# Subtracting the maxima in attention on TensorE, with sums on VectorE and norm offsets on GpSimd, in a two-layer transformer block

## The reference, cut to what matters

```
x = x + xattn0(layernorm(x), ctx)     # 16 heads of 16, 77 keys, softmax
x = x + ffn0(layernorm(x))            # layernorm(t + relu(t @ w1 + b1) @ w2 + b2) * gamma + beta
x = x + xattn1(layernorm(x), ctx)     # norms both inputs, one head of 256, softmax
x = x + ffn1(x_norm)                  # one of 8 matrices per position, chosen by a router
# xattn0, per head:
scores  = q @ k.T * 0.25
weights = softmax(scores)             # exp(scores - max) / sum
out     = weights @ v
# ffn1: idx = argmax_t(pe @ sign(tile_sigs).T); out = x_norm @ W[idx].T + b[idx]
```

## Time and profile before

| | us |
|---|---|
| median of 3 executions | 313.17 |
| lowest, highest | 312.77, 313.40 |
| span of the profiled execution | 314.0 |
| busy in it: TensorE | 267.9 |
| VectorE | 254.8 |
| ScalarE | 181.7 |
| GpSimd | 157.3 |

### The profile page before, as it was taken

How to read it: one execution, slowest core, us unless ns; L and a number is a source line. 1 busy time by engine, 2 the same in 40 slices (tenths; PEclk the granted TensorE clock), 3 DMA queues, 4 the chain that set the end, 5 groups by cost and what they waited for, 6 DMA issues and landing times.

```text
span 314.0 us, 6283 instructions
## 1 busy us (share of the span) xinstructions
PE 267.9 (85%) x2080; PEld 232.0 (74%) x2080; DVE 254.8 (81%) x664; ACT 181.7 (58%) x606; POOL 157.3 (50%) x157
## 2 busy tenths in 40 slices
PE   2954958977999998999999989999989999878960
PEld 2743937763999698689789959988878988666850
DVE  2998998972889999998997789899899986875640
ACT  2468628526368857478695857775754471454510
POOL 2253640275225878821652263268766653164854
PEclk9995596995999999999999999999999999997995
DMA  6922010240000372100001000011110000000222
GB/s 177 336 72 77 8 42 25 67 142 27 3 0 3 115 222 51 29 24 2 2 0 35 2 0 2 33 52 51 37 36 0 2 0 1 3 0 34 87 78 73
DMA packets 8797, 15.32 MB, mean 49 GB/s; under 512 B 1270, under 2 KB 6813, under 8 KB 8509
## 3 DMA queue, kind: packets, MB, share of 16 engines
q1 hardware_dynamic: 6845, 9.68, 9.2%
q0 software_dynamic: 1920, 5.25, 5.9%
HBM read 11.77 MB, written 3.15 MB: 48 GB/s over the span
## 4 chain that ended last, share of the span: by engine, by line
PE 37%; DVE 29%; issue 15%; POOL 12%; ACT 3%; DVEq 1%; DMA 1%; POOLq 0%; SPq 0%; ACTq 0%
PE PB L256 16%; PE PB L249 7%; PE PB L460 5%; DVE SM L598 3%; POOL SM L1220 3%; DVE SX L649 3%; DVE SM L609 3%; PE S L365 3%; PE S L377 2%; POOL out_x L1282 2%; DVE WD L837 2%; PE PB L327 2%; POOL RAW L1275 2%; DVE XN L701 2%; POOL HL L1254 2%
## 5 line engine op out<-in xcount | busy, mean ns | idle before, releaser
L1220 POOL TENSOR_TENSOR SM<-SM,nhalf 128x2 f32<-128x2 f32 x40 | 29.4, 737 | 98.4 <-DVE SM L604 97.9
L1060 ACT ACTIVATE E<-S,SX 128x77 f32<-128x77 f32 x128 | 39.5, 340 | 16.8 <-DVE SX L652 16.6
L256 PE MATMUL PB<-XTH,W1H 128*128 128x256 f32 x128 | 38.3, 299 | 3.9 <-issue 2.2
L1254 POOL TENSOR_TENSOR HL<-HF,HH 128x512 fp32r<-128x512 f32 x26 | 34.5, 1335 | 13.6 <-DVE HH L682 12.0
L1094 ACT ACTIVATE HF<-PB,cols 128x256 f32<-128x256 f32 x64 | 26.8, 473 | 20.9 <-PE PB L256 20.6
L256 PE MATMUL PB<-W2H,HH 128*128 128x256 f32 x128 | 37.9, 296 | 1.1 <-DVE HL L688 1.1
L256 PE MATMUL PB<-XTH,W1L 128*128 128x256 f32 x128 | 36.4, 284 | 0.0
L256 PE MATMUL PB<-XTL,W1H 128*128 128x256 f32 x128 | 36.4, 284 | 0.0
L256 PE MATMUL PB<-W2H,HL 128*128 128x256 f32 x128 | 35.8, 280 | 0.0
L256 PE MATMUL PB<-W2L,HH 128*128 128x256 f32 x128 | 35.8, 279 | 0.0
L460 PE MATMUL PB<-WD,XP 128*128 x120 | 29.9, 402 | 0.8 <-issue 0.8
(11 more groups left out here) (188 smaller groups left out, 778.3 us busy)
## 6 DMA issues: line engine op xcount, KB each, us to landing
RAW<-in_w SPq DMA_DIRECT2D x4, 512.0 KB, 5.0
WD<-in_WD SPq DMA_DIRECT2D x2, 1024.0 KB
X<-in_x SPq DMA_DIRECT2D x4, 256.0 KB, 7.1
x<-X SPq DMA_DIRECT2D x4, 256.0 KB, 2.2
bc<-in_rows SPq DMA_DIRECT2D x1, 768.0 KB, 7.3
RAW<-in_w_q SPq DMA_DIRECT2D x1, 256.0 KB, 4.2
Wo<-in_w_o SPq DMA_DIRECT2D x1, 256.0 KB, 7.8
RAW<-in_WqT SPq DMA_DIRECT2D x1, 256.0 KB
```

The source lines that it names most:

```text
L256: t = e.matmul(dst, a, b, start=first and j == 0, stop=last and j == n - 1)
L1060: t = e.activation(Ei[:, h * NK:(h + 1) * NK], P[:, at:at + NK], ACT.Exp, bias=SX[:, i, 2, k:k + 1], accum_out=SX[:, i, 1, k:k + 1])
L1220: e.tensor_tensor(sm(K, g, 9), sm(K, g, 8), nhalf[:, :], ALU.pow).then_inc(s["rs" + K], 1)
L1254: e.tensor_tensor(HL[:, hs, :], HF[:, (4 * g + j) % 3, :, :], f(HH[:, hs, :]), ALU.subtract).then_inc(s["hlP"], 1)
```

## The change

The negated maxima now go through TensorE. `smax` writes them straight from the reduction (`negate=True`) into NM, in columns 0 to 3 and 32 to 35 of a strip of 36. `tM` on TensorE transposes the strip into a bank of PB, `mt` on ScalarE copies it to SBUF as MT, and `sm` on TensorE adds MT times SEL (rows of ones for each head's 77 columns) onto the scores that are still in PSUM. Then one exponential over the whole piece reads PSUM and writes E, for every piece, and VectorE sums E for every piece. The offset of the norms A, B, C and D is made on GpSimd in two products (with -1, then with rs). The 15 offsets of the router FFN are loaded into registers at once (`starts`) on each of three engines, in the middle of the program. RR, NM and mask8 move into a part of XP. All five lists of calls are new, except that of SyncE.

```diff
-def by_head(i, a):
-    return a == 0
...
-        RR = sb("RR", [128, 2, 128])
+        MT = sb("MT", [36, 2, 128], F32R)
+        SEL = sb("SEL", [36, 4 * NK], F32R)
...
+        RR, NM, mask8 = two(XP[:, 1, 0, :]), XP[:, 1, 1, 0:172], XP[:, 1, 1, 176:184]
...
+        def load_starts(e, row, most, at):
+
+            values = nc.values_load_multi_w_load_instructions(EV[0:1, row, 0:NP], engines=[e.engine],
+                                                              min_val=0, max_val=most)[1]
+            for n in range(NP):
+                at[n] = values[n]
...
-                P = hold(("sc", g, i, a), ("S", k), ("ex", n + 1) if by_head(i, a) else ("sub", n // 2 + 1))
+                P = hold(("sc", g, i, a), ("S", k), ("ex", n + 1))
...
+            def tM(g, i, a, p):
+                n = 4 * g + 2 * i + a
+                w.wait_ge(s["m_id"], 1)
+                w.wait_ge(s["mx"], n + 1)
+                P = hold(("tM", g, i, a), ("B", p), ("mt", n + 1))
+                e.transpose(P[0:36, 0:128], NM[:, n % 4 * 36:n % 4 * 36 + 36], ident[:, :]).then_inc(s["tM"], 1)
+
+            def sm(g, i, a):
+
+                n = 4 * g + 2 * i + a
+                w.wait_ge(s["mt"], n + 1)
+                w.wait_ge(s["sel"], 2)
+                P = S4[:, place["sc", g, i, a][1], :]
+                for u in range(2):
+                    own = slice(32 * u, 32 * u + 4)
+                    t = e.matmul(P[:, u * 512:u * 512 + 4 * NK], MT[own, n % 2, :], SEL[own, :],
+                                 start=False, stop=True, skip_group_check=True)
+                t.then_inc(s["sm"], 1)
...
+            def starts():
+                w.wait_ge(s["route2"], 1)
+                load_starts(e, 0, 7 * 256, start)
...
-                    if n not in start:
-                        start[n] = e.value_load(EV[0:1, 0, n:n + 1], min_val=0, max_val=7 * 256)
...
-            keys(0); tA(0, 1); vmat(2); q(0, 3); vrep(0, 0); vrep(1, 1); sc(0, 0, 0, 0); sc(0, 0, 1, 1); r_scores(2)
...
+            keys(0); vmat(1); tA(0, 0); q(0, 2); vrep(0, 0); r_scores(1); sc(0, 0, 0, 0); sc(0, 0, 1, 1); tA(1, 2)
+            vrep(1, 3); tM(0, 0, 0, 0); sm(0, 0, 0); tM(0, 0, 1, 0); q(1, 2); sm(0, 0, 1); sc(0, 1, 0, 0)
...
-                e.scalar_tensor_tensor(out=sm(K, g, 10), in0=sm(K, g, 6), scalar=-1.0, in1=sm(K, g, 9),
-                                       op0=ALU.mult, op1=ALU.mult).then_inc(s["mr" + K], 1)
...
-            def scores(g, i, a):
+            def smax(g, i, a):
                 n = 4 * g + 2 * i + a
                 sv = two(bank("sc", g, i, a))[:, :, 0:4 * NK].rearrange("p u (h k) -> p u h k", k=NK)
-                hs = slice(8 * a, 8 * a + 8)
-                return n, sv, SX[:, i, 0, hs].rearrange("p (u h) -> p u h", u=2), hs
-
-            def smax(g, i, a):
-                n, sv, mx_, hs = scores(g, i, a)
                 w.wait_ge(s["sc"], n + 1)
+                w.wait_ge(s["d"], 6)
                 if g:
-                    w.wait_ge(s["rr"], n - 3)
+                    w.wait_ge(s["tM"], n - 3)
+                e.tensor_reduce(two(NM[:, n % 4 * 36:n % 4 * 36 + 64])[:, :, 0:4], sv, AX, ALU.max,
+                                negate=True).then_inc(s["mx"], 1)
+
+            def ssum(g, i, a):
+                n, hs = 4 * g + 2 * i + a, slice(8 * a, 8 * a + 8)
+                w.wait_ge(s["ex"], n + 1)
+                if g:
                     w.wait_ge(s["tE"], n - 3)
-                step(e.tensor_reduce(mx_, sv, AX, ALU.max))
-                settle()
-                if by_head(i, a):
-                    e.tensor_scalar(SX[:, i, 2, hs], SX[:, i, 0, hs], -1.0, None, ALU.mult).then_inc(s["neg"], 1)
-                else:
-                    e.tensor_tensor(E[:, i, a, 0:8 * NK].rearrange("p (u h k) -> p u h k", u=2, h=4), sv,
-                                    mx_.unsqueeze(3).to_broadcast([128, 2, 4, NK]),
-                                    ALU.subtract).then_inc(s["sub"], 1)
-
-            def ssum(g, i, a):
-                n, sv, mx_, hs = scores(g, i, a)
-                w.wait_ge(s["ex"], n + 1)
-                if not by_head(i, a):
-                    step(e.tensor_reduce(SX[:, i, 1, hs], E[:, i, a, 0:8 * NK].rearrange("p (h k) -> p h k", h=8),
-                                         AX, ALU.add))
-                    settle()
-                e.reciprocal(SX[:, i, 2, hs], SX[:, i, 1, hs]).then_inc(s["rc"], 1)
+                step(e.tensor_reduce(SX[:, i, 0, hs], E[:, i, a, 0:8 * NK].rearrange("p (h k) -> p h k", h=8),
+                                     AX, ALU.add))
+                settle()
+                e.reciprocal(SX[:, i, 1, hs], SX[:, i, 0, hs]).then_inc(s["rc"], 1)
...
+            def mt(g, i, a):
+                n = 4 * g + 2 * i + a
+                w.wait_ge(s["tM"], n + 1)
+                if n > 1:
+                    w.wait_ge(s["sm"], n - 1)
+                e.activation(MT[:, n % 2, :], bank("tM", g, i, a)[0:36, 0:128], ACT.Copy).then_inc(s["mt"], 1)
+
             def ex(g, i, a):
                 n = 4 * g + 2 * i + a
-                Ei = E[:, i, a, 0:8 * NK]
-                if by_head(i, a):
-                    P = bank("sc", g, i, a)
-                    w.wait_ge(s["neg"], n // 2 + 1)
-                    if g:
-                        w.wait_ge(s["tE"], n - 3)
-                    for h in range(8):
-                        at = h // 4 * 512 + h % 4 * NK
-                        k = 8 * a + h
-                        t = e.activation(Ei[:, h * NK:(h + 1) * NK], P[:, at:at + NK], ACT.Exp,
-                                         bias=SX[:, i, 2, k:k + 1], accum_out=SX[:, i, 1, k:k + 1])
-                else:
-                    w.wait_ge(s["sub"], n // 2 + 1)
-                    t = e.activation(Ei, Ei, ACT.Exp)
-                t.then_inc(s["ex"], 1)
+                w.wait_ge(s["sm"], n + 1)
+                if g:
+                    w.wait_ge(s["tE"], n - 3)
+                e.activation(two(E[:, i, a, 0:8 * NK]), two(bank("sc", g, i, a))[:, :, 0:4 * NK],
+                             ACT.Exp).then_inc(s["ex"], 1)
...
             def pc(b, r):
                 w.wait_ge(s["xtd"], 4 * b + min(r, 3) + 1)
-                w.wait_ge(s["route2"], 1)
                 if 8 * b + r > 1:
                     w.wait_ge(s["pr"], 8 * b + r - 1)
+                else:
+                    w.wait_ge(s["tE"], 32)
                 for v in range(1 if r == 7 else 2):
                     n = 2 * r + v
-                    if n not in start:
-                        start[n] = e.value_load(EV[0:1, 2, n:n + 1], min_val=0, max_val=7 * 128)
...
+                if K != "Y":
+                    e.tensor_tensor(sm(K, g, 11), sm(K, g, 6), minus[:, :], ALU.mult).then_inc(s["nm"], 1)
+                    minus_made[0] += 1
+                    w.wait_ge(s["rs" + K], g + 1)
+                    w.wait_ge(s["nm"], minus_made[0])
+                    e.tensor_tensor(sm(K, g, 10), sm(K, g, 11), sm(K, g, 9), ALU.mult).then_inc(s["mr" + K], 1)
```

270 lines of the change are left out of this document (146 added, 124 removed), and 2 rows, old and new, of the table SIGNALS.

## The result

| | before | changed |
|---|---|---|
| median of the runs, us | 313.28 (312.77 to 314.03, 4 runs) | 325.75 (322.65 to 327.83, 4 runs) |
| ratio, 95% interval | | 1.035, 1.029 to 1.040 |
| profiled span, us | 314.0 | 324.8 |

The change makes the kernel slower, by 12.5 us between the medians and by 10.9 us (3.5%) by the ratio. Forecast were 306.5, with 298 to 316 as the range; the time lies outside it. Ratios leave out slow executions (here that of 327.83 us), and the profiled executions of e3, e9, e16 and e18 further down were slow ones, 2 to 4 us above the median of their kernel. Measured again beside later runs the changed kernel took 326.09 us, ratio 1.040 (1.028 to 1.053).

What follows compares the result with a forecast made beforehand. TensorE was taken to bound the kernel from 80 us on, with waits before that and near the end. +7.7 - 13.5 + 3 - 4 = -6.8, from the profiled 314.0 to 307.2, given as 306.5 us; range 298 to 316.

Steps and rivals of the forecast that it cites:

- first 80 us: Early stretch where TensorE waits: three causes of waits relieved, less 2 us of new waits, -13.5 us (-7.5 to -20.3).
- new TensorE work, 22 pieces: Full stretch after the first second-FFN product: transposition and product pair cost 0.35 us a piece, +7.7 us (5.5 to 9.9).
- middle, chain and block of loads: Middle: waits at the second product in eight of 22 pieces, plus the one load of 15 offsets, +3 us (1 to 14).
- end: Last stage: offset waits before six passes go, -2; last group's attention waits go, -2; together -4 us (-1 to -5.5).
- (a): At 48.3 us TensorE idles 4.53 us, VectorE's router product stalling beside GpSimd's low part of the weights; removal -5.5 us.
- (b): At 69.3 and 73.6 us TensorE waits, GpSimd's gathers delaying low parts of the hidden layer; moving them gives -4 us.
- (c): At 24.4 and 30.6 us TensorE waits, with half clock after the first; half of 12 us taken back, -6 us.
- costed at nothing: VectorE's relief beyond 80 us and ScalarE's 47 us lie on engines that do not bound, so are worth nothing.
- Rival 2: Slower: TensorE waits at the second product for ScalarE, deciding from 0.45 us a piece; 323 to 324 us, chance 0.16.
- Rival 1: The port: offset waits pass on to normalizations as GpSimd holds VectorE, early gains shrink; 311 us, chance 0.14.
- signs named ahead: Right if: no long router product, low parts before gathers, first product at 66 to 70 us, short copy waits, last group unheld.
- signs of "wrong": Half clock over 10 us before 60 us; TensorE under 18 of 20 us between 100 and 240; normalizations with waits inside.

Runs made afterwards that it cites:

- e3: Kernel before with only GpSimd's first two low parts of the hidden layer moved ahead of the eight gathers; 317.2 us, ratio 1.002.
- e9: Changed kernel with VectorE and ScalarE loading offsets one at a time through the middle, TensorE in front of its passes; 317.5 us, ratio 1.017.
- e16: e9 with the router's two large VectorE steps and TensorE's rank product back where they stood before the change; 325.0 us, ratio 1.022.
- e18: e9 without the 64 products that add the maxima, transpositions and ScalarE's copies kept; 307.9 us, ratio 0.980.
- e12: Changed kernel, unedited, measured again as reference on the chip of later runs; 326.1 us, ratio 1.040.
- e19: e9 unedited, measured again as reference on the chip of later runs; 317.4 us, ratio 1.024.
- e11: e9 without the transpositions of the maxima, their copies and the added products, maxima computed but unused; 305.2 us, ratio 0.979.
- e2: Kernel before with the block of 15 offset loads on TensorE, VectorE and ScalarE in place of single loads; 320.4 us, ratio 1.012.
- e14: Kernel before with VectorE and ScalarE loading offsets one at a time in the middle, not ahead of the passes; 316.7 us, ratio 1.001.
- e1: Changed kernel with the block of loads undone on all three engines, each offset loaded in front of its pass; 327.4 us, ratio 1.035.
- e17: e9 with no maxima at all: no reductions, transpositions, copies or added products; 305.9 us, ratio 0.982.
- e13: e9 with the softmax of the kernel before, new order and spread loads kept; 324.0 us, ratio 1.023.
- e5: New softmax put into the order of the kernel before, offsets loaded one by one; 346.2 us, ratio 1.087.

## Why the prediction was wrong, step by step

| step | forecast | measured |
|---|---|---|
| first 80 us | -13.5 (-7.5 to -20.3) | -12.4 (82.6 to 70.2 in e12; -10.4 in the first profile) |
| new TensorE work, 22 pieces | +7.7 (5.5 to 9.9) | +9.0 (e19 against e11) |
| middle, chain and block of loads | +3 (1 to 14) | +11.7: the block 10.9 to 11.0 (e12 against e9, e19), 0.7 for the rest |
| end | -4 (-1 to -5.5) | +2.1 in e12, +0.5 in the first profile |

The measured column adds up to 10.4 us for e12, whose span is 324.4 against 314.0. It is split by subtraction between kernels, so each term carries what a part varies by: the start up to 8.7 us between the kernels of this order, the end some two. Of the 17.2 us between the forecast sum of -6.8 and the measured 10.4 the middle has 8.7, the end 6.1, the work 1.3 and the start 1.1.

**The step that failed is "the middle".** It said that waits at the second product "and the one load of 15 offsets with its 30 register instructions (a load and two of them now let TensorE wait 0.41 us) give +3". Two things were wrong in it. The row it went by has the wait that was left on TensorE behind one small load; the block is 15 times that register work, 0.22 us a time, in one piece, behind a load of 1.65 us. Times fifteen the same row would have given 6 us. And what comes behind the stops was left out: TensorE's own 4.49 us are followed by 5.3 us at a granted clock of 0.50, and VectorE, which executes the same block, stands for 6.26 us, behind which TensorE waits 2.20 us and runs at 0.53 for 3.6 us. The two waits and what the lower clock takes in the two stretches (half of 5.3, 0.47 of 3.6) are 4.5 + 2.2 + 2.65 + 1.7, an estimate of 11.0 us, and the block measured 10.9. The other half of the step was right: TensorE waited for ScalarE's copy 1.3 us in all over 32 pieces in the changed kernel.

**The start** was right in size, and the waits that it named did go: 4.53 (a), 2.19 and 2.16 (b), 4.66 and 3.22 us (c) before; in the changed kernel TensorE has no wait above 1.6 us between 10 and 80 us, in e12 none above 0.9 between 20 and 80. Which of the named moves did it is open. -5.5 was for the router's product that would no longer stall (a): e16 puts it back, but without the GpSimd work beside it, so the term stays untested. -4 was for the low parts ahead of the gathers (b): e3 has the first product 7.3 us earlier from that alone, and nothing of it in the time. That the gain of the start stays in the changed kernel while e3 loses it has to do with the rest of the order; which steps, no run tells. Of cause (c) the waits came out fully and the clock in part: the granted clock from 20 to 40 us is 0.63 where it was 0.57, and 0.83 in e12. That all of these waits went and yet only 10 to 12 us were gained fits the new work that stands in the same stretch, ten of the 32 pieces and the V product; no run splits it.

**The end** failed too: forecast were -4, measured +0.5 and +2.1. "The offset loads -2" is about right for the kernel before, where taking them out of the end gave 1.8 (e2) and 1.1 us (e14). The other -2 was for TensorE's waits at the last group's attention. They are gone, the longest of 1.59 us among them, but TensorE's routed passes have new ones:

```profile
284.24 1.99 PE L485 MATMUL PB<-WD,XP 128*128 x8 [2.17 <-ACT XP L1171]
...
307.96 6.28 PE L485 MATMUL PB<-WD,XP 128*128 x28 [1.40 <-DVE X L776]
```

Added up, TensorE's waits behind the last W2H product are 4.0 us before and 4.1 now. Moreover, in the new order the last stage starts later: before, two passes of the routed products stand ahead of the last group's second FFN matrix; now the first comes at 277.1, behind its last product at 276.1. That is the likely reason for 50 us of end in all kernels of this order, argued from the two traces and not tried alone. Without the loads' removal it would have been 61.4 (e1).

**The work** was right within its bounds, at 0.41 us against 0.35 a piece.

**VectorE and ScalarE "costed at nothing"** was half right. The reductions are hidden (e17). But the relief was not worth nothing: the old softmax in the new order costs about as much as the 12 us of new products (e13). Relief on an engine that does not bound was what paid for the new work there. On ScalarE that relief was 19 us of busy time, not the 47 of the forecast's sum.

**The rivals.** Rival 2, slower through the chain at the second product, had the sign and nearly the time (323 to 324), and not the mechanism: the waits there were below 0.05 us a piece on the mean, and its 0.45 us were not reached. That its time fits is luck: it has 9 us of waits that did not come, and lacks the block. In the old order it came true in part (e5, 4.8 us of waits for the copy). Rival 1's sign of a handed-on wait is there in the first profile. GpSimd, VectorE and TensorE:

```profile
32.75 2.36 POOL L1245 TENSOR_TENSOR W2L<-RAW,W2H 128x1024 fp32r<-128x1024 f32 x1 [0.30 <-ACT W2H L1026]
...
32.77 2.50 DVE L651 TENSOR_SCALAR XN<-X,SM 128x256 f32<-128x256 f32 x1
...
35.32 1.11 PE L332 MATMUL PB<-ident,XN 128*128 128x128 f32 x4 [1.54 <-DVE XN L651]
```

From 90 to 250 us the same line takes 0.40 us on the mean; this one starts with a GpSimd instruction beside it and ends 0.16 us after that. In e12, the same kernel, it starts at 27.98 us, in a gap of GpSimd between 27.79 and 28.10, and takes 0.38. The rule of the Trainium skill (SBUF — State Buffer, Who interferes with whom) would have it so for a scalar operation in a fast mode, and both traces agree. TensorE waited 1.54 us for it, and the first W2H product of that profile comes 2.0 us later than that of e12. The chance of 0.17 for slower was too low: the middle's own upper bound of 14 against a taken value of 3 said that a loss was near, since 306.5 + 11 is 317.5, and the range ended at 316.

Of the signs named ahead, the low parts, the absent router product, the short wait for ScalarE's copy and the last group's attention without its wait came out right; the first product at 72.2 missed 66 to 70, in e12 by 0.2 us; and all three signs of "wrong" stood there: the normalization of 2.50 us, TensorE below 18 of 20 us at 140 to 160 and 180 to 200, which is the block, and a clock of 0.63 on the mean from 20 to 40, which is half level for some 15 of the 20 us.
